# Attention over image rows: q, k and the score buffers interleaved by two rows, score columns in the order of the relative rounds, sums and normalisation on four rows at a time

## The reference, cut to what matters

```
q, k, v = (conv1x1(wq, x), conv1x1(wk, x), conv1x1(wv, x))   # each (n, h, c, i, w)
qk  = einsum('nhcij,nhciw->nhijw', q, k) / D
qrq = einsum('nhcij,chjw->nhijw', q, rq) / D
krk = einsum('nhcij,chjw->nhijw', k, rk) / D
weight = softmax(qk + Gq * qrq + Gk * krk, axis=3)            # over j
out = einsum('nhijw,nhciw->nhcij', weight, Gv1 * v) + einsum('nhijw,chjw->nhcij', weight, Gv2 * rv)
x = x + conv1x1(wo, out)
```

## Time and profile before

| | |
|---|---|
| median of 3 runs | 7482.63 us (7476.99 to 7494.4) |
| the profiled execution | 7491.67 us, span 7489.7 us |
| busy: TensorE, its weight loads, VectorE, ScalarE, GpSimd | 89%, 68%, 72%, 66%, 33% of the span |
| projection, about 190 to 1490 us | TensorE busy all the time |
| attention, about 1500 to 5870 us | TensorE 97%, ScalarE 86%, VectorE 82%, GpSimd 50% from 2000 to 5000 us |
| combine and experts | the rest |

### The profile page before, as it was taken

How to read it: one execution, slowest core, us unless ns; L and a number is a source line. 1 busy time by engine, 2 the same in 40 slices (tenths; PEclk the granted TensorE clock), 3 DMA queues, 4 the chain that set the end, 5 groups by cost and what they waited for, 6 DMA issues and landing times. The chain is left out here.

```text
span 7489.7 us, 279833 instructions
## 1 busy us (share of the span) xinstructions
PE 6636.5 (89%) x106442; PEld 5093.8 (68%) x106442; DVE 5358.8 (72%) x20905; ACT 4975.0 (66%) x11171; POOL 2487.3 (33%) x1267
## 2 busy tenths in 40 slices
PE   4999999979999999999999999999999766676558
PEld 3555555568888888888888888888888433232258
DVE  5444444448888888888887888878888688898820
ACT  0666665558888888888888888888888334333300
POOL 0000000025455545545544554544554323232110
PEclk6999999969999999999999999999999888798755
DMA  7566666546666666666666666666665667586422
GB/s 217 202 202 203 204 204 205 191 87 123 122 132 124 120 132 127 128 118 131 124 120 134 124 123 128 130 121 125 127 128 112 202 230 234 190 266 199 142 97 95
DMA packets 804192, 1146.42 MB, mean 153 GB/s; under 512 B 101344, under 2 KB 562784, under 8 KB 800928
## 3 DMA queue, kind: packets, MB, share of 16 engines
q1 hardware_dynamic: 613600, 842.59, 49.8%
q10 hardware_dynamic: 188352, 285.27, 10.3%
q0 software_dynamic: 1024, 2.09, 0.1%
HBM read 708.04 MB, written 421.56 MB: 151 GB/s over the span
## 5 line engine op out<-in xcount | busy, mean ns | idle before, releaser
L789 POOL TENSOR_TENSOR att_scores<-att_scores,att_inverse 128x1024 f32<-128x1024 f32 x1024 | 1998.8, 1952 | 2168.9 <-DVE att_inverse L737 2168.6
L696 ACT ACTIVATE att_scores<-att_scores,att_negmax 128x128 f32<-128x128 f32 x8192 | 2505.4, 392 | 20.0 <-issue 17.8
L613 PE MATMUL att_ps<-att_own 32*128 32x128 f32 x16384 | 2391.6, 440 | 122.0 <-DMA att_own<-qk 67.3
L752 DVE CUSTOM_DVE_ANT_0 att_scores<-att_ps,att_scores 128x128 f32<-128x128 f32 x8192 | 1817.0, 289 | 813.6 <-PE att_ps L613 809.4
L613 PEld LDWEIGHTS att_ps<-att_own 32*128 32x128 f32 x16384 | 2089.7, 329 | 439.1 <-issue 251.0
L602 PE MATMUL att_ps<-att_qk,att_rs 32*128 32x64 f32 x32768 | 2140.3, 280 | 50.9 <-DMA att_qk<-qk 37.0
L602 PEld LDWEIGHTS att_ps<-att_qk,att_rs 32*128 32x128 f32 x32768 | 1994.8, 193 | 57.0 <-issue 50.0
L655 PE MATMUL att_ps<-att_scores,att_rv 128*16 128x64 f32 x32768 | 1384.5, 331 | 9.8 <-issue 8.0
L735 DVE TENSOR_REDUCE att_total<-att_scores 128x8 f32<-128x1024 f32 x1024 | 1241.9, 1213 | 0.0
L689 ACT ACTIVATE att_scores<-att_ps 128x1024 f32<-128x1024 f32 x1024 | 1037.8, 1014 | 287.2 <-PE att_ps L602 228.4
L655 PEld LDWEIGHTS att_ps<-att_scores,att_rv 128*16 128x16 f32 x32768 | 1125.3, 119 | 26.1 <-issue 16.4
(11 more groups left out here) (147 smaller groups left out, 5180.9 us busy)
## 6 DMA issues: line engine op xcount, KB each, us to landing
qk<-proj_qk_out ACTq DMA_DIRECT2D x64, 2048.0 KB, 9.8
att_qk<-qk SPq DMA_DIRECT2D x512, 256.0 KB, 4.7
att_own<-qk SPq DMA_DIRECT2D x1024, 128.0 KB, 4.1
proj_x<-in_x_dram SPq DMA_DIRECT2D x128, 512.0 KB, 4.4
v_t<-proj_v_out ACTq DMA_DIRECT2D x64, 1024.0 KB, 12.6
att_vt<-v_t SPq DMA_DIRECT2D x256, 256.0 KB, 4.9
att_v<-att_att_v SPq DMA_DIRECT2D x1024, 64.0 KB, 3.5
att_r<-att_att_r SPq DMA_DIRECT2D x1024, 64.0 KB, 2.6
```

The lines of the kernel that those rows point to most:

```text
L613: return pe.matmul(ps[:, g, r * W:(r + 1) * W], own[half][32 * g:32 * g + 32, 1, :, at], own[half][32 * g:32 * g + 32, 0, :, at], start=Tr ...
L696: last = act.activation(scores[v % BUFS][:, i, :], scores[v % BUFS][:, i, :], ACT.Exp, bias=negmax[v % BUFS][:, i:i + 1], scale=-1.0)
L752: last = dve.tensor_tensor_reduce(out=scores[v][:, i, :], in0=ps[:, 2 * (p % 2) + r // HR, (r % HR) * W:(r % HR + 1) * W], in1=scores[v][: ...
L789: pool.tensor_tensor(piece(scores[v], p), piece(scores[v], p), piece(inverse[v], p).unsqueeze(3).broadcast_to([P, 2, HR, W]), ALU.mult).th ...
```

## The change

In `project` the copy from PSUM writes pairs of rows interleaved: element (b, w, i) at b * 256 + w * 2 + i, b the pair, i the row in it. `qk`, `own` and `scores` in SBUF take the same shape, with `PAIR = 2` rows side by side. The columns j of a score row stand in the order of the relative rounds (`by_place`, `by_column` translate). The reduction of `sums_of` and the multiplication of `normalise` work on four rows in two instructions each instead of eight rows in one.

```diff
+PAIR = 2
@@ project
-                    at = (j // 4) * ROWS // 2
-                    act.activation(qk_out[u][:, j % 4, :].rearrange("o (w i) -> o i w", i=ROWS)[:, at:at + ROWS // 2, :],
-                                   qk_ps[:, j % 4].rearrange("o (i w) -> o i w", w=W), ACT.Copy).then_inc(qk_read, 1)
+                    at = (j // 4) * BANK
+                    act.activation(qk_out[u][:, j % 4, at:at + BANK].rearrange("o (b w i) -> o b i w", w=W, i=PAIR),
+                                   qk_ps[:, j % 4].rearrange("o (b i w) -> o b i w", i=PAIR, w=W), ACT.Copy).then_inc(qk_read, 1)
@@ attend
-        qk = [s.sb(f"qk{b}", [P, IU // ROWS, JG, ROWS]) for b in range(2)]
-        own = [s.sb(f"own{b}", [P, 2, W, ROWS]) for b in range(2)]
+        qk = [s.sb(f"qk{b}", [P, IU // PAIR, JG, PAIR]) for b in range(2)]
+        own = [s.sb(f"own{b}", [P, 2, ROWS // PAIR, W, PAIR]) for b in range(2)]
-        scores = [s.sb(f"scores{v}", [P, IU, W]) for v in range(BUFS)]
+        scores = [s.sb(f"scores{v}", [P, IU // PAIR, W, PAIR]) for v in range(BUFS)]
+        def row(v, i):
+            return scores[v][:, i // PAIR, :, i % PAIR]
+        def by_place(columns):
+            return columns.rearrange("r (g q j) -> r q g j", g=G, q=QUARTERS)
+        def by_column(places):
+            return places.rearrange("r (q g j) -> r g q j", g=G, q=QUARTERS)
+        def four(tile, p, x):
+            first = row_of(p, HR * x)
+            return tile[:, first:first + HR].rearrange("w (b i) -> w b i", i=PAIR)
+        def score_four(v, p, x):
+            first = row_of(p, HR * x) // PAIR
+            return scores[v][:, first:first + HR // PAIR, :, :]
@@ load_qk
-                                 d["qk"][...].rearrange("r (b g x) -> r b g x", g=G, x=ROWS * JG)[:, :, g, :])
+                                 d["qk"][...].rearrange("r (b g x) -> r b g x", g=G, x=PAIR * JG)[:, :, g, :])
@@ own_score
-                return pe.matmul(ps[:, g, r * W:(r + 1) * W], own[half][32 * g:32 * g + 32, 1, :, at], own[half][32 * g:32 * g + 32, 0, :, at],
+                return pe.matmul(ps[:, g, r * W:(r + 1) * W], own[half][32 * g:32 * g + 32, 1, at // PAIR, :, at % PAIR], by_place(own[half][32 * g:32 * g + 32, 0, at // PAIR, :, at % PAIR]),
@@ sums_with_v, sums_with_r: the moving operand
-                        ... scores[v % BUFS][:, i, :]
+                        ... by_column(row(v % BUFS, i))
-                        ... scores[v % BUFS][:, :, j]
+                        ... scores[v % BUFS][:, :, b * JB * G + g * JB + jj, :]
@@ read_relative
-                act.activation(scores[o % BUFS][:, :, :].rearrange("w i (g j) -> w i g j", g=G)[:, :, pair:pair + 2, t // 2 * JB:(t // 2 + 1) * JB],
-                               ps[:, 4:6, :].rearrange("w g (j i) -> w i g j", i=IU), ACT.Copy).then_inc(rel_read, 1)
+                act.activation(scores[o % BUFS][:, :, place:place + 2 * JB, :],
+                               ps[:, 4:6, :].rearrange("w g (j b i) -> w b (g j) i", b=IU // PAIR, i=PAIR), ACT.Copy).then_inc(rel_read, 1)
@@ exp_half and add_and_largest use row(v, i) in place of scores[v][:, i, :]
@@ sums_of
-                dve.tensor_reduce(piece(total[v], k), piece(scores[v], k), AX_X, ALU.add).then_inc(summed, 1)
-                dve.wait_ge(summed, PIECES * u + k + 1)
+                for x in range(2):
+                    dve.tensor_reduce(four(total[v], k, x), score_four(v, k, x).rearrange("w b j i -> w b i j"), AX_X, ALU.add).then_inc(summed, 1)
+                dve.wait_ge(summed, HALVES * u + 2 * k + 2)
@@ normalise
-                pool.tensor_tensor(piece(scores[v], p), piece(scores[v], p), piece(inverse[v], p).unsqueeze(3).broadcast_to([P, 2, HR, W]),
-                                   ALU.mult).then_inc(normed, 1)
+                for x in range(2):
+                    pool.tensor_tensor(score_four(v, p, x), score_four(v, p, x), four(inverse[v], p, x).unsqueeze(2).broadcast_to([P, HR // PAIR, W, PAIR]),
+                                       ALU.mult).then_inc(normed, 1)
```

More of the change, by code:

```diff
@@ L440, in piece @@
             at = HR * (p % (PIECES // 2) // 2)
-            if len(tile.shape) == 2:
-                return tile[:, first:first + 2 * ROWS].rearrange("w (x r) -> w x r", x=2)[:, :, at:at + HR]
-            return tile[:, first:first + 2 * ROWS, :].rearrange("w (x r) j -> w x r j", x=2)[:, :, at:at + HR, :]
+            return tile[:, first:first + 2 * ROWS].rearrange("w (x r) -> w x r", x=2)[:, :, at:at + HR]
+        def four(tile, p, x):
[4 more added lines that the diff above has]
+            return scores[v][:, first:first + HR // PAIR, :, :]
         def later(eng, semaphore, value):
@@ L484, in load_qk @@
                     sp.dma_start(qk[k % 2][32 * g:32 * g + 32, :, :, :].rearrange("r b j i -> r b (j i)"),
-                                 d["qk"][bass.ds(h * 32, 32), pixel:pixel + IU * W].rearrange("r (b g x) -> r b g x", g=G, x=ROWS * JG)[:, :, g, :]).then_inc(qk_loaded[k % 2], 16)
+                                 d["qk"][bass.ds(h * 32, 32), pixel:pixel + IU * W].rearrange("r (b g x) -> r b g x", g=G, x=PAIR * JG)[:, :, g, :]).then_inc(qk_loaded[k % 2], 16)
             def load_own(h, k, half):
@@ L489, in load_own @@
                 for g in range(G):
-                    sp.dma_start(own[half][32 * g:32 * g + HD, :, :, :].rearrange("r t w i -> r t (w i)"),
+                    sp.dma_start(own[half][32 * g:32 * g + HD, :, :, :, :].rearrange("r t b w i -> r t (b w i)"),
                                  d["qk"][bass.ds(h * 32, 32), pixel + g * CHUNK:pixel + (g + 1) * CHUNK].rearrange("(t r) x -> r t x", t=2)).then_inc(own_loaded[half], 16)
@@ L637, in sums_with_v @@
                     if b == 0:
-                        pe.wait_ge(normed, PIECES * u + PIECES)
+                        pe.wait_ge(normed, HALVES * u + HALVES)
                     later(pe, v_read, FILLS * u + b)
@@ L642, in sums_with_v @@
                         i = 16 * b + 4 * g + r
-                        last = pe.matmul(ps[32 * g:32 * g + HD, 6, r * W:(r + 1) * W], vt[i // HROWS][:, i % HROWS, :], scores[v % BUFS][:, i, :],
+                        last = pe.matmul(ps[32 * g:32 * g + HD, 6, r * W:(r + 1) * W], vt[i // HROWS][:, i % HROWS, :], by_column(row(v % BUFS, i)),
                                          start=True, stop=True, tile_position=(0, 32 * g))
@@ L654, in sums_with_r @@
                         j = g * JG + b * JB + jj
-                        last = pe.matmul(ps[32 * g:32 * g + HD, 7, jj * IU:(jj + 1) * IU], rv[:, j, :], scores[v % BUFS][:, :, j],
+                        last = pe.matmul(ps[32 * g:32 * g + HD, 7, jj * IU:(jj + 1) * IU], rv[:, j, :], scores[v % BUFS][:, :, b * JB * G + g * JB + jj, :],
                                          start=True, stop=True, tile_position=(0, 32 * g))
@@ L683, in read_relative @@
             def read_relative(u, o, t):
-                pair = 2 * (1 - t % 2)
+                place = t // 2 * JB * G + (1 - t % 2) * 2 * JB
                 act.wait_ge(rel_done, ROUNDS * u + t + 1)
@@ L695, in exp_half @@
                     i = row_of(p // 2, p % 2 * HR + r)
-                    last = act.activation(scores[v % BUFS][:, i, :], scores[v % BUFS][:, i, :], ACT.Exp, bias=negmax[v % BUFS][:, i:i + 1], scale=-1.0)
+                    last = act.activation(row(v % BUFS, i), row(v % BUFS, i), ACT.Exp, bias=negmax[v % BUFS][:, i:i + 1], scale=-1.0)
                 last.then_inc(exped, 1)
@@ L751, in add_and_largest @@
                     i = row_of(p, r)
-                    last = dve.tensor_tensor_reduce(out=scores[v][:, i, :], in0=ps[:, 2 * (p % 2) + r // HR, (r % HR) * W:(r % HR + 1) * W], in1=scores[v][:, i, :],
+                    last = dve.tensor_tensor_reduce(out=row(v, i), in0=ps[:, 2 * (p % 2) + r // HR, (r % HR) * W:(r % HR + 1) * W], in1=row(v, i),
                                                     scale=-1.0, scalar=LARGEST, op0=ALU.add, op1=ALU.min, accum_out=negmax[v][:, i:i + 1])
@@ L774, in _ @@
             for half in range(2):
-                dve.memset(own[half][:, :, :, :], 0.0).then_inc(cleared, 1)
+                dve.memset(own[half][:, :, :, :, :], 0.0).then_inc(cleared, 1)
             dve.memset(ps[:, 6:8, :], 0.0).then_inc(cleared, 1)
```

## The result

The changed kernel takes 7646.14 us (median of four, 7635.7 to 7649.01) against 7483.95; the ratio is 1.0213 (95% interval 1.0201 to 1.0225). The forecast was 7270, faster by 2.9%: the sign was wrong. The profiled execution has a span of 7643.7 us.

The account below looks back on a forecast made before the run. TensorE was taken to bound attention at 8.06 us a pair. From 7491.67 us, 364 saved by a 7.35 us pair, less 140 at head ends and 3 at the start, gave 7270; own range 7130 to 7400, all cases 7130 to 7850.

Parts of the forecast that it names:

- rival D: Attention: TensorE waiting each pair could lower its granted clock below 0.97 and stretch its 6.6 us; given no chance.
- the 364 us that the pair was to give: Middle of attention: a pair of pieces shortened by 0.71 us, over 512 pairs.
- Step of 2 free on VectorE and ScalarE: Exponentials, adding rows and reduction in attention: accessing every second element costs 0 extra ns an element.
- rival A: Step of 2 costs VectorE 0.71 and ScalarE 0.98 ns an element, like larger steps; 8530 us, chance 0.20.
- rival C: Step of 2 costs a small 0.15 to 0.3 ns an element on VectorE; 7500 to 7790 us, chance 0.10.
- TensorE's pair of 6.6 us: Attention: own scores 0.28 and r products 0.45 us faster a piece, leaving TensorE 3.30 us a piece.
- VectorE sets the pair at 7.35: Attention: VectorE, at 7.32 us a pair with split reductions, becomes the bound; pair 7.35 instead of 8.06 us.
- the sign of it: Predicted evidence in the new profile: VectorE busy over 92% in the middle of attention.
- Head ends at 140 us: Ends of 15 heads: own loads arrive later behind a longer queue, 9.3 us more each, 140 us lost.
- the 5 us more of queue time for a qk load: SyncE's queue: four DMAs of 1024 runs instead of 256 take 5 us more a unit, from between 0 and 8.8.
- Projection hidden: Projection: line 336's copy may drop from 1102 to about 600 ns, gaining nothing as ScalarE waits 422 us for TensorE.
- Rival B: qk loads hold SyncE 8.8 us longer, so late own loads eat the gain; about 7410 to 7550 us, chance 0.12.

Follow-up runs that it names:

- e8: Kernel before, layout and loads untouched, with ScalarE making the read of every odd round three times so that TensorE waits; 8484 us.
- e4: Only the scores' half of the change (rows in pairs, round order, split sums and normalisation), q and k as in the kernel before; 7553 us.
- e9: Changed kernel with qk loads cut to two of 64 rows from unit 3 on, result not the reference's; 7193 us.
- e14: Kernel before with only SyncE's order changed: second-half own load ahead of the qk load, next head's gain loads four units earlier; 7609 us.
- e18: Kernel before with only the next head's gain loads asked for four units earlier, qk load at its old place; 7426 us.
- e15: Changed kernel with second-half own load ahead of the qk load and next head's gain loads four units earlier; 7523 us.
- e3: Only the q and k half of the change (interleaved by two, qk loads in 256-byte runs), scores as in the kernel before; 7499 us.
- e17: e12 with the qk load one step later on SyncE, behind the v load; 7348 us, fastest that leaves nothing out.
- e7: Changed kernel with the four DMAs of each qk load spread over two pieces; 7634 us.
- e13: Changed kernel with qk loads reading the same bytes in 1 KB runs instead of 256 bytes, data landing in wrong order; 7520 us.
- e16: e4 with second-half own load ahead of the qk load and next head's gain loads four units earlier; 7749 us.
- e12: e3 with second-half own load ahead of the qk load and next head's gain loads four units earlier; 7427 us.
- e1: Changed kernel with eight products with v made a second time behind the r products of every piece; 7758 us.
- e2: Changed kernel with repeated v products, four behind an even piece and sixteen behind an odd one; 7816 us.
- e5: Changed kernel plus one wide constant matmul a piece, 160 columns behind even and 448 behind odd pieces; runs between 7830 and 8031 us.
- e6: e4 plus one wide matmul a piece, 96 columns behind even and 384 behind odd pieces; 7689 us.

## Why the prediction was wrong

**The step that failed is rival D.** "At half the clock TensorE would again be the bound and busy, so I give it no case of its own" had the first half right and the conclusion wrong. TensorE is busy at half the clock and gets the full clock back, but then it waits again and loses it again: e8 shows this cycle bare. At 1.2 GHz a pair takes 10.90 us, not 7.11, so a half-clock microsecond loses 1 - 7.11 / 10.90 = 0.35. Of 1574 us that is 547, against 282 x (1 - 7.94 / 11.5) = 87 before. The sum had put this term at nothing; the difference comes to 460 us by this estimate, more than the 364 us that the pair was to give. The case should have been priced so from the start; the row of what half the clock does was missing, but twice 6.6 us bounded it.

**What D named was only part of it.** It had TensorE's waits of each pair lower the clock. They do in e8 and in e4, but in the changed kernel most falls (57 of 97) come behind issue stops, and in e9, with most of those gone and the waits for ScalarE kept, the clock is 0.93.

**The second miss was a term that the sum did not have:** TensorE's stops without a named cause. Issue waits rose by 148 us (179.5 against 31.4), besides the falls of the clock behind them.

The account: pace at full clock 512 x (7.11 - 7.94) = -425 us; clock +460; issue +148; own loads +27 (94.3 against 67.3). That is +210 where attention became 4431 - 4275 = 156 us longer; the terms overlap, by some 54 us. Priced the same way, e9's 453 us are some 310 of clock (half-clock time from about 1600 to 720 us) and 130 of issue waits (180 to 49), but the two overlap, and what the loads cost otherwise these runs don't part. That it is the qk load that makes the stops is shown by e9 and e14 against e18; that it does so by holding up instructions is inferred.

**Step of 2 free on VectorE and ScalarE:** right on VectorE, nearly so on ScalarE. 288 ns against 289 in line 774; the reduction takes 677 for 512 elements against a median of 1212 for 1024 contiguous, 1.04 ns for each element between them; ScalarE 408 against 392, 0.13 ns an element, where rival A had 0.71 and more. So the rule of the Trainium skill ("Advanced Engine Details and Errata", SBUF Cachelines: two hits on a 16-byte line are full speed) agrees with the trace, and "Vector Engine (DVE) Microarchitecture Reference", 5.2 Measured stream behaviour, with its runs of adjacent words, does not for float32 here. The choice on which the sign was said to hang held, and the sign was wrong all the same. That 7646 lies within rival C's 7500 to 7790 is chance: its price of 0.15 to 0.3 ns on VectorE is not there.

**TensorE's pair of 6.6 us:** too high. The 0.28 us a piece for own scores came as said (2.22 to 1.94); r gave 0.69, not 0.45. Its pieces without the waits are about 3.1 us (3003.19 to 3006.25), so about 6.1; r went to 20 ns a record, past the 28 I took. The 8.06 of the kernel before was read from one pair; over more of them it is 7.94 to 7.99.

**VectorE sets the pair at 7.35:** the size was near (7.11), the engine was wrong: from 3029 to 3058 us ScalarE is busy 28.5 of 29 us, VectorE 26.9. From 3000 to 4000 us VectorE is busy 817 us, not over 920 as the sign of it had been. The split reductions cost 0.14 us a piece (2 x 677 ns against 1212) and are hidden: VectorE still waits 866.7 us for own scores in front of line 774.

**Head ends at 140 us:** mis-sized. Own waits rose by 27 us, the longest from 5.5 to 10.2. The step in it that failed is the 5 us more of queue time for a qk load: from the first of its four DMAs to the end of the last it holds the queue a median 3.7 us against 1.9. But taking the queue's chain apart gave 123 us in the changed kernel (e15), where the half-clock time fell as well, from 1612 to 1336 us of attention.

**Projection hidden:** right; the copy fell from 1102 to 637 ns and ScalarE's wait for TensorE rose from 422 to 603.5. qk landings: 6.0 us, as said.

**Rival B** (the queue eats the gain) was right in naming the qk loads and wrong in the way: they do it through TensorE's stops and the clock (e9), with few late operands.

## What to carry to other kernels

If an edit makes TensorE wait where it was busy, price it at both clock levels before trusting the gain: the pair at 2.4 GHz, TensorE's own time at 1.2 GHz, and a share between. A strided operand can hide what the clock costs (r products before: 1.34 us at 2.4 GHz, 1.38 at 1.2), and the kernel without it loses more to a half clock. Look at the issue waits of a TensorE with many small instructions; in e14 loads that stand together cost there although their data was early. And test the order of the loads with the edit: the interleave of q and k gave nothing by itself (e3) and 1.8% with another order (e17); the order of the gains alone gives 0.8% (e18) in the kernel before.

## Not expected of the hardware

- The clock went with waits of a fraction of a piece: 0.83 in e8 for 450 us of waits in 3000.
- The half-clock stretches last differently: on average 17 us in the changed kernel, 4 in e8, 9 in e3. Leaving the fillers aside, it goes with the layout of the scores: 16 to 19 us in every kernel with rows in pairs (after, e4, e7, e9, e13, e15, e16), 4 to 11 in every one with contiguous rows (before, e3, e8, e12, e14, e17, e18). With more v products it is 9 and 7 (e1, e2), with a large wide matmul 38 and 23 (e5, e6). Why, stays open.
- The same bytes in a quarter of the runs are worth 126 us, though own-load waits stay as they were (75 us against 69 in the table's window; e13).
